# A selective scan whose input products are shared out anew: 19 of 64 turns to ScalarE and TensorE, 12 to GpSimd

## The reference

```python
# layer 1, on the layer norm of x: (2, 1024, 256), 16 states per channel
x_dbl = einsum('bld,kd->blk', x, W_xproj)           # 64 for delta, 16 for B, 16 for C
delta = softplus(einsum('blr,dr->bld', x_dbl[..., :64], W_dt) + b_dt)
deltaA = exp(delta[..., None] * A)                  # the decay
BX = delta[..., None] * Bmat[:, :, None, :] * x[..., None]
h = dA * h + bx                                     # for each token in turn
y = einsum('bdn,bn->bd', h, c)                      # then + D * x, and the residual
# layer 2, on the layer norm of that: each token goes to one of 32 experts (top 1),
# whose weights are the ternary weights times the expert's 0/1 mask (256 x 256 each)
out = where(top1_idx == e, (x @ (w_scaled * mask_e).T) * top1_w, out)
```

## Time and profile before

| | us |
|---|---|
| median of 3 runs | 352.99 (352.36 to 355.46) |
| profiled execution | 352.72 |
| its span, first to last instruction | 350.9 |
| VectorE busy | 296.9 |
| GpSimd busy | 268.9 |
| TensorE busy | 246.6 |
| ScalarE busy | 159.4 |
| first multiply of turn 0 starts at | 30.22 |
| last scan (turn 63) starts at | 239.26 |

### The profile page before, as it was taken

How to read it: one execution, slowest core, us unless ns; L and a number is a source line. 1 busy time by engine, 2 the same in 40 slices (tenths; PEclk the granted TensorE clock), 3 DMA queues, 4 the chain that set the end, 5 groups by cost and what they waited for, 6 DMA issues and landing times.

```text
span 350.9 us, 3847 instructions
## 1 busy us (share of the span) xinstructions
PE 246.6 (70%) x1188; PEld 141.9 (40%) x1188; DVE 296.9 (85%) x368; ACT 159.4 (45%) x216; POOL 268.9 (77%) x153
## 2 busy tenths in 40 slices
PE   0765698977688997689999787979710006999740
PEld 0522244423235653345655244544500003899630
DVE  2999999999999999999999979995998792566750
ACT  1475574365865565565455453330760400544210
POOL 0493988999798999999999969999056580377772
PEclk9995599998989999999999899899955556999885
DMA  7436899999996999998999538750003346898400
GB/s 240 127 121 197 213 325 330 382 380 360 340 306 191 308 316 304 325 312 278 334 301 322 203 115 299 234 181 6 0 0 121 150 180 224 308 292 258 155 2 0
DMA packets 36499, 79.32 MB, mean 226 GB/s; under 512 B 5043, under 2 KB 15805, under 8 KB 36480
## 3 DMA queue, kind: packets, MB, share of 16 engines
q1 hardware_dynamic: 23888, 63.68, 55.3%
q10 hardware_dynamic: 9776, 9.09, 8.2%
q0 software_dynamic: 2816, 6.32, 4.8%
HBM read 64.07 MB, written 17.09 MB: 231 GB/s over the span
## 4 chain that ended last, share of the span: by engine, by line
DVE 47%; issue 19%; PE 14%; POOL 7%; DMA 6%; ACT 5%; ACTq 0%; POOLq 0%; SPq 0%; DVEq 0%
DVE xs_sb L773 17%; DVE bank L768 10%; PE bank L1025 7%; DMA out_dram<-cb,to_token 4%; DVE wT L897 4%; POOL out_dram L446 4%; DMA x_sb<-in_L_attn_x_dram 2%; ACT dA L551 2%; POOL xs_sb L395 2%; PE bank L993 2%; DVE st L793 2%; PE bank L1121 1%; POOL mask_sb L387 1%; DVE xn L702 1%; DVE st L681 1%
## 5 line engine op out<-in xcount | busy, mean ns | idle before, releaser
L395 POOL TENSOR_TENSOR xs_sb<-xs_sb,cb 128x1024 f32<-128x1024 f32 x64 | 150.0, 2367 | 7.4 <-DVE xs_sb L773 6.1
L1025 PE MATMUL bank<-xs_sb,cst 128*128 128x512 f32 x256 | 127.4, 624 | 1.3 <-ACT xn L556 0.7
L773 DVE TENSOR_TENSOR_SCAN xs_sb<-dA,bank 128x1024 f32<-128x1024 f32 x44 | 100.6, 2287 | 1.5
L1025 PEld LDWEIGHTS bank<-xs_sb,cst 128*128 128x128 f32 x256 | 48.8, 197 | 45.8 <-issue 35.9
L768 DVE TENSOR_TENSOR bank<-bank,rows 128x1024 f32<-128x1024 f32 x44 | 53.3, 1211 | 0.1
L993 PE MATMUL bank<-bc,pick 96*128 96x512 bf16 x88 | 29.2, 419 | 33.6 <-DVE xs_sb L773 33.6
L551 ACT ACTIVATE dA<-rows,a_neg 128x1024 f32<-128x1024 f32 x44 | 49.5, 1139 | 1.0 <-DVE rows L741 0.5
L446 POOL DMA_INDIRECT out_dram<-cb,to_token x32 | 31.9, 997 | 23.4 <-DVE cb L916 16.7
L387 POOL TENSOR_TENSOR xn<-xn,rows 128x1024 f32<-128x1024 f32 x16 | 37.7, 2357 | 5.5 <-DMA xn<-bc_rows 5.4
L773 DVE TENSOR_TENSOR_SCAN xs_sb<-bank,xn 128x1024 f32<-128x1024 f32 x16 | 36.3, 2270 | 0.3 <-ACT bank L551 0.2
L656 ACT ACTIVATE xn<-bank 128x1024 f16<-128x1024 f16 x16 | 16.3, 1023 | 42.5 <-PE bank L1145 42.5
(11 more groups left out here) (141 smaller groups left out, 330.0 us busy)
## 6 DMA issues: line engine op xcount, KB each, us to landing
cb<-bc_rows SPq DMA_DIRECT2D x64, 512.0 KB, 5.4
sorted_tokens<-wT SPq DMA_DIRECT2D x32, 257.0 KB, 9.2
xn<-bc_rows SPq DMA_DIRECT2D x16, 512.0 KB, 7.3
mask_sb<-_L_ffn_expert_masks_dram ACTq DMA_DIRECT2D x32, 256.0 KB, 6.4
xs_sb<-sorted_tokens SPq DMA_DIRECT2D x7, 1028.0 KB, 8.4
x_sb<-in_L_attn_x_dram SPq DMA_DIRECT2D x4, 512.0 KB, 7.9
mask_sb<-bc_rows SPq DMA_DIRECT2D x4, 512.0 KB, 5.5
xs_sb<-sorted_tokens SPq DMA_DIRECT2D x2, 514.0 KB, 4.3
```

Source lines behind the costliest of these rows:

```text
L395: pool.tensor_tensor(prod[:, j, :], h[:, j, :], cb[:, j, :], ALU.mult).then_inc(s_prod, 1)
L773: dve.tensor_tensor_scan(h[:, j, :], decays, bx, 0.0, ALU.mult, ALU.add).then_inc(s_scan, 1)
L1025: mm = pe.matmul(yacc[:, c * HC:(c + 1) * HC], ident, prod[:, j, c * HC:(c + 1) * HC], start=first, stop=last, skip_group_check=True)
```

## The change

Three kinds of turn in place of two. Of each 16 turns of the four groups, GpSimd now has n = 1, 7, 13 (in the last group 5, 9, 13), 12 turns in all in place of 20. ScalarE and TensorE have n = 5, 9, 11, 15 in the first group, 3, 5, 9, 11, 15 in the second and third and 1, 3, 7, 11, 15 in the last, 19 turns. The other 33 stay with VectorE (44 before).

For the turns of the new kind, B and u are first turned so that tokens lie on partitions: `turn_b` and `b_T_out` once for each batch, `turn_u` and `u_T_out` twice for each group (four f32 transposes and one 128 x 512 copy each). In such a turn ScalarE makes u*B with eight copies of 128 x 128 that each take the B of their tokens as a per-partition scale (`act_bx(k+2)` in its step k, after `decay(k+1)` and ahead of `mask_out`). TensorE turns the eight pieces back into `b_ps` (`turn_bx(k+1)` in its step k, in the place of `b_rows`), and VectorE only scans.

Besides: `product` now works in place on h, in a ring of six (`HELD`) in place of a ring of four for h and one for the products, so GpSimd no longer waits for `sums`, and a scan waits for the sums of turn k-6. The loads of B for GpSimd have one buffer up to turn 51, and the first GpSimd turn is 1.

```diff
-POOL_STATES = (2, 5, 8, 11, 14)
+HELD = 6
+POOL_STATES = ((1, 7, 13), (1, 7, 13), (1, 7, 13), (5, 9, 13))
+ACT_STATES = ((5, 9, 11, 15), (3, 5, 9, 11, 15), (3, 5, 9, 11, 15), (1, 3, 7, 11, 15))
...
+        BT_AT = {0: 0, 10: 1}
+        UT_AT = {2: (0, 0), 3: (0, 1), 12: (1, 0), 14: (1, 1), 19: (2, 0), 20: (2, 1), 46: (3, 0), 47: (3, 1)}
...
-                if k >= RING:
-                    pool.wait_ge(s_sum, k - 3)
-                pool.tensor_tensor(prod[:, j, :], h[:, j, :], cb[:, j, :], ALU.mult).then_inc(s_prod, 1)
+                here = h[:, k % HELD, :]
+                pool.tensor_tensor(here, here, cb[:, j, :], ALU.mult).then_inc(s_prod, 1)
...
+            bx(pool_turns[0])
             for k in range(TURNS):
                 if k + 2 in pool_turns:
                     bx(k + 2)
...
+            def act_bx(k):
+                i, g, n = of_act[k], k // N, k % N
+                act.wait_ge(s_utsb, LH * (g + 1))
+                act.wait_ge(s_btsb, g // DH + 1)
+                if i >= 2:
+                    act.wait_ge(s_bready, of_psum[act_turns[i - 2]] + 1)
+                for c in range(LB):
+                    ins = act.activation(u_b_T[:, i % 2, c, :], u_T(g)[:, c, :], ACT.Copy,
+                                         scale=b_T[:, g // DH * LB + c, n:n + 1])
+                ins.then_inc(s_abx, 1)
...
                 if k + 1 < TURNS:
                     decay(k + 1)
+                if k in BT_AT:
+                    b_T_out(BT_AT[k])
+                if k in UT_AT:
+                    u_T_out(*UT_AT[k])
+                if k + 2 in act_turns:
+                    act_bx(k + 2)
...
+                    if k not in act_turns:
+                        dve.tensor_tensor(bx, bx, u[:, dh, b * L:(b + 1) * L], ALU.mult).then_inc(s_bx, 1)
...
-                if k >= RING:
-                    dve.wait_ge(s_prod, k - 3)
+                if k >= HELD:
+                    dve.wait_ge(s_sum, k - HELD + 1)
...
+            def turn_bx(k):
+                i = of_act[k]
+                pe.wait_ge(s_abx, i + 1)
+                pe.wait_ge(s_scan, k - 1)
+                for c in range(LB):
+                    mm = pe.transpose(b_ps[k % 2][:, c * P:(c + 1) * P], u_b_T[:, i % 2, c, :], ident)
+                mm.then_inc(s_bready, 1)
```

More of the change, by code:

```diff
@@ L105, in selective_scan_then_routed_ternary_ffn @@
         flat = "p a l -> p (a l)"
-        before = prod[:, :, :].rearrange(flat)
+        before = h_and_prod[:, 4 * L:8 * L]
         wx_nat = before[0:96, 1024:1024 + D]
@@ L257, in selective_scan_then_routed_ternary_ffn, with mask_half, u_T @@
         sign_ps = bank[:, 1, :]
-        pool_turns = [k for k in range(TURNS) if k % N in POOL_STATES]
+        pool_turns = [k for k in range(TURNS) if k % N in POOL_STATES[k // N]]
+        act_turns = [k for k in range(TURNS) if k % N in ACT_STATES[k // N]]
         of_pool = [sum(1 for p in pool_turns if p < k) for k in range(TURNS + 1)]
-        of_dve = [k - of_pool[k] for k in range(TURNS + 1)]
+        of_act = [sum(1 for p in act_turns if p < k) for k in range(TURNS + 1)]
+        of_psum = [k - of_pool[k] for k in range(TURNS + 1)]
+        of_dve = [of_psum[k] - of_act[k] for k in range(TURNS + 1)]
         masks_done = MASK_FROM + E
+        def mask_half(k):
+            return (of_pool[k] - of_pool[masks_done]) % 2
         def b_buffer(k):
-            half = of_pool[k] % 2
             if k < masks_done:
-                return yT[:, 1, half, :]
+                return yT[:, 1, 0, :]
+            half = mask_half(k)
             return mask_sb[:, 2 * half:2 * half + 2, :, :].rearrange("p j h i -> p (j h i)")
+        def u_T(g):
+            return yT[:, 0 if g == 1 else 1, 1, :].rearrange("p (c d) -> p c d", c=LB)
         ROUTER_AT, CENTRE_AT, SIGNS_AT = MASK_FROM, MASK_FROM + 2, MASK_FROM + 4
@@ L968, in _, with turned_b, turned_u @@
                 delta_in(m, bank[:, m, :])
+            def turned_b(k):
+                return sum(1 for at in BT_AT if at < k)
+            def turned_u(k):
+                return sum(1 for at in UT_AT if at < k)
             def prepare(k):
@@ L994, in b_rows, with turn_b, turn_u @@
                                    bc3[:, cols], start=True, stop=True)
+                mm.then_inc(s_bready, 1)
+            def turn_b(b):
+                pe.wait_ge(s_low, LH * (b + 1))
+                for c in range(LB):
+                    mm = pe.transpose(w_ps[:, 2 * N * c:2 * N * c + 2 * N], xd[lanes, c * P:(c + 1) * P], ident[lanes, lanes])
+                mm.then_inc(s_btps, 1)
+            def turn_u(g, c):
+                b, dh = g // DH, g % DH
+                pe.wait_ge(s_u, LH * g + c + 1)
+                for t in range(4):
+                    at = b * L + c * HC + t * P
+                    mm = pe.transpose(w_ps[:, t * P:(t + 1) * P], u[:, dh, at:at + P], ident)
+                mm.then_inc(s_utps, 1)
+            def turn_bx(k):
+                i = of_act[k]
+                pe.wait_ge(s_abx, i + 1)
+                pe.wait_ge(s_scan, k - 1)
+                for c in range(LB):
+                    mm = pe.transpose(b_ps[k % 2][:, c * P:(c + 1) * P], u_b_T[:, i % 2, c, :], ident)
                 mm.then_inc(s_bready, 1)
@@ L1048, in _ @@
                     pe.wait_ge(s_bc3, LH + 4)
-                if k + 1 < TURNS and k + 1 not in pool_turns:
+                if k + 1 in act_turns:
+                    turn_bx(k + 1)
+                elif k + 1 < TURNS and k + 1 not in pool_turns:
                     b_rows(k + 1)
@@ L1053, in _ @@
                 if k >= LAG:
-                    sums(k - LAG, (k - LAG) % RING, first=(n == LAG), last=(n == LAG - 1))
+                    sums(k - LAG, (k - LAG) % HELD, first=(n == LAG), last=(n == LAG - 1))
                 if RING <= n < RING + LB:
@@ L1059, in _ @@
                 prepare(k)
+                if k in BT_AT:
+                    pe.wait_ge(s_xnsb, 2 * DH * LH)
+                    if k:
+                        pe.wait_ge(s_low, B * LH)
+                    turn_b(BT_AT[k])
+                if k in UT_AT:
+                    pe.wait_ge(s_btsb, turned_b(k))
+                    if turned_u(k):
+                        pe.wait_ge(s_utsb, turned_u(k))
+                    pe.wait_ge(s_abs, 2 + sum(1 for at in SOFT_AT if at < k))
+                    if k > MASK_FROM:
+                        pe.wait_ge(s_wt, k - MASK_FROM)
+                    turn_u(*UT_AT[k])
                 if k == ROUTER_AT:
@@ L1099, in _ @@
             for k in range(TURNS - LAG, TURNS - 1):
-                sums(k, k % RING)
+                sums(k, k % HELD)
             pe.wait_ge(s_scan, TURNS - 1)
@@ L1106, in _ @@
             turn_x1(3)
-            sums(TURNS - 1, (TURNS - 1) % RING, last=True, apart=True)
+            sums(TURNS - 1, (TURNS - 1) % HELD, last=True, apart=True)
             for c in range(LH):
```

48 lines of the change are left out of this document (34 added, 14 removed).

## The result

The changed kernel takes 376.46 us (median of four runs, 375.81 to 379.43) against 353.86 (352.36 to 355.46) for the kernel before: ratio 1.065, 95% interval 1.058 to 1.073. A later measurement of both gave 1.058 (1.051 to 1.065). The change makes the kernel 6% slower. The profiled execution has a span of 373.8 us, 22.9 more than before.

A forecast was written before the change was run, and what follows sets the result against it. VectorE was taken to bound the kernel before; 352.7 - 13.6 (multiplies) - 2.9 (old waits) + 33.5 (new waits) - 0.6 (end) = 369.1 us, stated as 368 by positions; own range 359 to 376, 8 in 10 351 to 378.

The forecast's parts named there:

- the ring: Steps 20 to 51: TensorE's transposes, sums, skip and mask, ScalarE's mask copy, decay and eight copies; 7.9 us per two turns.
- Scans 25 and 27: Second group, worked-out stretch: scan 27 starts 8.8 us after scan 25, where 5.65 were possible; 3.2 us lost.
- Eight copies: ScalarE's 128 x 128 copies with per-partition scale for one turn: 0.30 us each, 2.4 us; 1.6 with plain spacing.
- TensorE alone is a little too slow for such a pair: Groups two and three, two steps with skips and one ScalarE turn: TensorE needs 6.09 us, VectorE 5.65.
- The gain: VectorE drops 11 multiplies of 1.24 us, 13.6 us; old waits, mostly for GpSimd inputs, credited at 2.9 us.
- GpSimd holds: Per group of 16 turns, GpSimd needs 44.1 us against VectorE's 45.2, so it stays just under.
- The last product and sums come 0.6 us sooner: Behind the last scan: product and sums end 0.6 us sooner, since GpSimd lags less.
- The waits, 33.5 us: VectorE's new waits over all 64 turns: groups 7.6, 10, 9.2 and 6.7 us, sum 33.5.
- the delta step behind turn 5: First group: projection for the soft part stands behind TensorE's wait in step 4 and comes 2.8 us late.
- taking the positions (368.0) over the sum (369.1): Total by position, last scan ending at 257.5 not 241.55, gave 368.1, stated as 368; summing terms gave 369.1.
- The clock falls as well: Rival: TensorE's clock falls after its waits for ScalarE at about eight places, 9 us more, 377; chance 0.07.
- VectorE stays the bound: Rival: the loop fits into 5.65 us, so VectorE sets the pace; 340.3, up to 345 us; chance 0.15.

The follow-up runs named there:

- experiment 1: Changed kernel with ScalarE's eight copies made up to four turns ahead, not two: turns 222.2 us, ratio 1.024 to the kernel before.
- experiment 3: Changed kernel with a constant scale of 0.5 in the eight copies, not the column of B: turns 224.2 us, ratio 1.036 to the kernel before.
- experiment 5: Changed kernel with ScalarE's copy of the turned mask one step later: turns 223.4 us, ratio 1.031 to the kernel before.
- experiment 7: Combined version: changed kernel, first group as before, copies four (last group three) turns ahead, mask copy later, last group's u earlier: turns 211.7 us, ratio 1.000 to before.
- experiment 10: Kernel of experiment 7 without TensorE's matmuls of skip and residual, so the output lacks both: turns 210.0 us, one execution.
- experiment 8: Kernel before, with in-place products, ring of six, and ScalarE turns only at 7, 11, 15 of the last group: turns 210.1 us, ratio 0.996 to before.
- experiment 11: Kernel of experiment 8 with the last group's u turned one step earlier and turn 55's copies three turns ahead: turns 211.0 us, ratio 0.991 to before.
- experiment 9: Changed kernel with eight extra bf16 matmuls on TensorE in step 4, ahead of the wait for turn 5's copies: turns 228.9 us, one execution.

## Why the prediction was right

The forecast of 368.0 us was for the likeliest case, in which the ring binds, and that mechanism came. The size was less good: the measured 376.46 is 8.5 us above it, just outside the case's own range (359 to 376) and inside the range for 8 in 10 (351 to 378).

- **The ring.** Predicted 7.9 us, 8.3 where the signs are turned as well; measured 8.39. Scans 25 and 27: predicted 8.8 apart, measured 8.77. Experiments 1, 3 and 5 each changed one link, and the distance followed each: 5.81, 8.02 and 6.52. This is shown. So is the remark that TensorE alone is a little too slow for such a pair, by the 6.52 of experiments 5 and 7 and the 5.63 of experiment 10.
- **Eight copies.** Predicted 2.4 us, 2.5 to TensorE's start; measured 2.44 at 47.09 and 141.17 - 138.69 = 2.48. One copy lasts 388 ns in the trace, and eight take 0.305 us each (2.44 / 8), where 0.30 was estimated from the rows. That 19 such turns lose time comes by way of the ring and not by ScalarE's total (busy 160.1 of 235 us); three such turns behind the masks cost nothing (ratios 0.996 and 0.991 in experiments 8 and 11).
- **The gain.** Eleven multiplies and the old waits were credited in full. VectorE's single waits of over 0.1 us add up to 37.6 us in the trace, near the 39.0 that the balance leaves with these credits, so they hold to within 1.4 us. That GpSimd holds was right (its only new wait on VectorE is turn 1's 1.01 us, predicted 1.2). "The last product and sums come 0.6 us sooner" was wrong: 109.3 us before and after.
- **The waits, 33.5 us: mis-sized.** They measured 39.0. The term furthest off is the first group's, 7.6 against 11.2, and in it the delta step behind turn 5: its wait was predicted at 2.8 us and measured 4.78, and its start came 8.5 us later than before and not some 5. I had step 4 wait, but let the sums behind it run at full clock. Experiment 9 gives back 3.4 us of this group's waits (3.9 less the 0.5 of the load) and 1.3 of the second's in the execution with TensorE kept busy; that wait is 3.09 there. Without them the groups stand at 7.8 and 10.5, where 7.6 and 10 were predicted. The third and last group took 0.5 of it back, so over all groups it is 4.2 us.
- **The rest of the 8.5 us.** 368.0 to 376.5 is 5.5 from the waits, 0.6 from the end, 1.1 from taking the positions (368.0) over the sum (369.1), 0.5 from a first multiply at 30.76 and not 30.22, and 0.8 more around the span (376.46 - 373.8 = 2.7, before 1.8).
- **The rivals.** "The clock falls as well" was right in kind and priced at 9 us, where 4.2 went with the filler, in an execution without the falls at three places of the first group (0.57, 0.74 and 0.66); behind the waits of 1.66 us in the masked steps the clock stayed at 1.00. That its 377 us is nearer to the measured time than the forecast's 368 is luck: half of its price came, the rest of the gap is made of other terms. It should have stood in the forecast as a term and not beside it at 0.07, since the kernel before already showed a fall from 1.00 to 0.50 behind such a wait. "VectorE stays the bound" needed the ring under 5.65 us. Even the combined version does not bring VectorE to its bound: its second group takes 54.2 us, where 51.78 - 3 x 1.24 - 0.2 = 47.9 would be the bound.
- **Still open.** What else holds the combined version's second and third groups above their bound. TensorE's work is part of it (2.0 us of the 6.3 in the second group), and a late row of B for GpSimd is another (1.86 us at turn 17 by its trace). How the rest is shared by the clock, GpSimd's loads and the longer round through ScalarE, the runs don't part.

## What to carry to other kernels

Work moved to an idle engine cost nothing here only where it could lie beside that engine's waits (the three turns of experiment 8: turns of 210.1 us against 211.3). Ask what its queue holds before and behind, and add up the ring engine to engine. If the ring is longer than the bottleneck's own time, expect its excess in the time, whatever the busy shares say (here 8.39 against 5.65 us for scans 25 and 27, with no engine over 84%). Before giving such work up, cut the ring at one link (make the product earlier, or consume the other engine's result one step later): here either cut gave back 10 us or more of 22. Even then the best use was small: three turns where nothing else closes a ring, for less than 1%.
